# Two conditioned layers, fp32, on one core: another order of work where level 0 gives way to level 1, plain fp32 edge layers, and VectorE's fold step ahead of layer 1's in level 1

## The chip, the cores and the metric

One core of a Trainium2 chip. The metric is the device time of one launch in microseconds. The time before is a median of 933.09 us over 3 runs (the lowest 931.63, the highest 933.41).

## The reference, cut to what matters

```python
def _layer(x, style, w, b, mw, mb, typ):
    s = style @ mw.T + mb
    weight = SCALE * w * s[:, None, :, None]
    demod = lax.rsqrt(jnp.sum(weight * weight, axis=(2, 3)) + EPS)
    weight = weight * demod[:, :, None, None]
    ...
x = x + _L0_ffn_ref(_L0_cond_ref(x, cond_512, ...), L0_ffn_A, L0_ffn_B, L0_ffn_Wr)
x = x + _L1_ffn_ref(_L1_cond_ref(x, cond_512, ...), qweight, scales, zeros, bias)
```

x is 32 samples of 64 channels by 1024 positions, in fp32. The four layers of a level are of the types same, upsample (and blur), same, (blur and) downsample. Each of the two levels runs four modulated convolutions of three taps along the positions (64 channels in and out) and then a product along the positions: level 0's is a gated low-rank adapter (the top 16 of 64 experts by score), level 1's a matrix of 4-bit weights, unpacked as scale times nibble minus zero.

## The kernel before, in words

**Pairs.** The 32 samples are worked on in 16 pairs; a pair fills 128 rows in the products along positions. Level 0 handles pairs 0 to 15 and level 1 the same samples again as 16 to 31. `c` in the code is the pair whose convolutions are computed, `i` or `f` the pair whose product is; in level 0 `c = i + 1`, in level 1 `c = i + 3` (AHEAD). Level 0 stores its result in `x_after_first`, from which level 1 loads it again.

**Two parts for one fp32.** Most products run in the faster fp32r form on operands that are cut in two, hi and lo, and three matmuls (hi by hi, hi by lo, lo by hi) make one product (`products`, L175). ScalarE makes the hi part, VectorE the lo part by a subtraction (`low`, L164), and TensorE waits for the lo part. So nearly every step of a pair is a relay: TensorE, ScalarE (`act_...`), VectorE (`dve_...`), TensorE (`pe_...`).

**Steps of one pair c.** `split`: x into `x_hi`, `x_lo`. `layer1`: the first convolution into `conv_ps`, then `h_hi`, `h_lo`. `fold_start`, `fold3`, `fold2`: the weights of layers 2 to 4 are multiplied into one stationary operand for each sample, `v` (ScalarE `v_hi`, VectorE `v_lo`) then `r` (out of `fold_ps`, `r_hi` L755, `r_lo` L760) then `e` (`e_hi` L788 to L791, `e_lo` and two copies). `cond`: the product of `h` and `e`, four taps of three matmuls for each of the two samples, then ScalarE writes it out (L860). `pe_fold2(c)` waits for VectorE's `r_lo` of c and for `e` of c-1; `pe_cond(c, a)` for `e` of c and `h_lo`; `pe_layer1(c, a)` for VectorE's `x_lo` of c and for ScalarE's write of `cond(c-1, a)`.

**The edges.** The folded operand is wrong at the first and the last position of a sample. Those are computed apart, for all 32 samples together and one time in a level, by four small layers in a row: `edge_tensor` layer 0 to 3 on TensorE (widths 192, 128, 192 and 32 columns), and `edge_vector` step 0 to 4 on VectorE around them. Level 0 does that at the start of the program with raw fp32 operands (`head_edge_tensor`, `head_edge_vector`: one matmul for each product). Level 1 does it in the change of level with three fp32r matmuls for each product; its turn, w2 and down weights are cut in hi and lo by ScalarE (`edge_tiles`), GpSimd (`blurred_lo`) and VectorE (`raw_lo`), and each of its steps 0 to 3 ends with two VectorE instructions for the hi and lo part (`parts`). Step 0 needs the few end positions of all samples in `x_edge`: 30 samples come by DMA, the last two, which exist last, by eight small VectorE copies (`edge_copies`, L279 to L288), which raise `edges_copied`.

**Who waits for `edges_copied`.** SyncE, before it issues the three loads of scales, zeros and bias (L1228, 512 KB each), behind which the loads of `x_in` for pair 19 and all later ones stand in its queue (L1166, L1167); GpSimd's queue, before the loads of the first three residuals (L1280, 512 KB each); ScalarE, before nibbles 6 and 7.

**Order.** The order of all engines is written out by hand. The change of level is the stretch between level 0's loop and level 1's: pairs c = 17, 18 and 19 get their convolutions, level 0's last product runs in two halves (`pe_adapter_out`), and the 4-bit matrix is unpacked by VectorE and ScalarE in eight parts (`dve_nibbles`, `act_nibbles`). After it, `second_step(i)` runs for i = 17 to 28: on TensorE layer 1 of sample 0, transposes, layer 1 of sample 1, fold 3, a third of the quantized product, fold 2, two thirds of the product, `cond`. On VectorE it is:

```python
dve_turn(v, i, bufs)
dve_layer1(v, c, 0, bufs)
dve_fold3(v, c, bufs)
dve_layer1(v, c, 1, bufs)
dve_fold2(v, c, bufs)
```

Of the kernel before, what the change touches and what calls it, by code (L numbers as in the profile page):

```python
# [8 lines left out]
F32R = mybir.dt.float32r  # L9
# [11 lines left out]
P = 128  # L21
# [14 lines left out]
AHEAD = 3  # L36
# [4 lines left out]
def program(nc, t):  # L41
    with ExitStack() as outer:
# [52 lines left out]
        S.tiles_cleared = sem("tiles_cleared")  # L95
        S.sides_cleared = sem("sides_cleared")
# [138 lines left out]
        def setup_edges(stack, L, s):  # L235

            T = lambda n, s, d=F32: tensor(stack, f"L{L}_{n}", s, d)
            s.w2_raw, s.turn = T("w2_raw", [P, 2 * P]), T("turn", [P, 8, C])
            s.x_edge = T("x_edge", [P, 2, B, 4])
            if not L:  # L240
                s.edge = [T("side0", [P, 2, 4, B]), T("side1", [P, 2, 3, B]), T("side2", [P, 2, 4, B])]
                s.scaled, s.turned = T("side_scaled", [P, 2, 3, B]), T("side_turned", [P, 2, 2, 2, B])
                return
            s.w2_hi, s.w2_lo = T("w2_hi", [P, 2, P], F32R), T("w2_lo", [P, 2, P], F32R)
            s.turn_hi, s.turn_lo = T("turn_hi", [P, 4, P], F32R), T("turn_lo", [P, 4, P], F32R)
            s.down_hi, s.down_lo = T("down_hi", [P, 5 * C], F32R), T("down_lo", [P, 5 * C], F32R)
            s.edge, s.edge_hi, s.edge_lo = [None] * 4, [None] * 4, [None] * 4
            for i in range(2):
                n = 4 - i
                s.edge[i], s.edge_hi[i], s.edge_lo[i] = T(f"side{i}", [P, 2, n, B]), T(f"side_hi{i}", [P, 2, n, B], F32R), T(f"side_lo{i}", [P, 2, n, B], F32R)  # L250
                s.edge[i + 2], s.edge_hi[i + 2], s.edge_lo[i + 2] = s.edge[i], s.edge_hi[i], s.edge_lo[i]
            s.scaled = T("side_scaled", [P, 2, 3, B])
# [148 lines left out]
        def head_edge_tensor(pe, s, layer):  # L401
# [10 lines left out]
            pe.wait_ge(S.edge_ready, layer + 1)  # L412
            if layer in (0, 2):
                if layer:
                    pe.wait_ge(S.w2_loaded, 16)
                raw = s.w2_raw if layer else s.w1_raw
                last = sums(sides(prod_ps[0], 3), [raw[:, i * P:(i + 1) * P] for i in range(2)], [part(layer, i, 3) for i in range(2)])
            elif layer == 1:
                pe.wait_ge(S.turn_blurred, 1)
# [11 lines left out]
        def head_edge_vector(v, s, step):  # L431
# [9 lines left out]
            if step == 0:  # L441
                v.wait_ge(S.edges_loaded, 16)
                for side in range(2):
                    last = V.tensor_tensor(s.edge[0][:, side, :, :], s.x_edge[:, side, :, :].rearrange("p b j -> p j b"),
                                           wide(style_tab[:, 0, :], 4), ALU.mult)
                last.then_inc(S.edge_ready, 1)
            if step == 1:
                v.wait_ge(S.edge_done, 1)
                v.wait_ge(S.tables_ready, 1)
                v.wait_ge(S.sides_cleared, 1)  # L450
                link(v, V.scalar_tensor_tensor(out=six(s.scaled), in0=blocks(prod_ps[0], 6), scalar=SCALE, in1=wide(scale1, 6), op0=ALU.mult, op1=ALU.mult))
# [4 lines left out]
            if step == 2:  # L456
                v.wait_ge(S.edge_done, 2)
# [1443 lines left out]
```

## Time and profile before

| | us |
|---|---|
| median of 3 runs (931.63 to 933.41) | 933.09 |
| the profiled execution's own time | 933.7 |
| its span | 932.0 |
| TensorE busy in it | 918.5 |
| weight loads (PEld) busy | 826.8 |
| VectorE, ScalarE, GpSimd busy | 494.2, 410.0, 92.1 |

The 1.7 us between the profiled execution's time and its span lie before and after the first and the last instruction. In a timeline the ends of matmuls are modelled and overlap the next start, so the time that a group of matmuls takes is read from its first start to the start of what follows. "L" in front of a number is a line of the kernel before; in a tile name of the profile, "L_" stands for a buffer of either level.

### The profile page before, as it was taken

How to read it: one execution, taken by the hardware profiler on the slowest of the kernel's cores; microseconds unless marked ns; L12 is line 12 of the kernel's file. 1: busy time of each engine (PE TensorE's matmuls, PEld its weight loads, DVE VectorE, ACT ScalarE, POOL GpSimd, SP SyncE). 2: the span in 40 equal slices, each digit the busy share in tenths (PEclk: the TensorE clock that was granted, in tenths of full speed). 3: DMA queues.
4: the chain of work that ended last, by engine and by line, in shares of the span. 5: the costliest groups of instructions: out<-in, count | busy, mean ns of one | idle time of the engine just before them, and what ended most of it. 6: DMA issues, size and time to landing. Idle time of an engine off the chain costs nothing.

```text
span 932.0 us, 14652 instructions
## 1 busy us (share of the span) xinstructions
PE 918.5 (99%) x5032; PEld 826.8 (89%) x5032; DVE 494.2 (53%) x1071; ACT 410.0 (44%) x764; POOL 92.1 (10%) x115
## 2 busy tenths in 40 slices
PE   7899999999999999999999999999999999999998
PEld 6789899899899898898898898988998899998998
DVE  6795345245245244254344365587566556666555
ACT  4863333343244144233234234486555565555540
POOL 0000000000000000000000020321211121111121
PEclk9999999999999999999999999999999999999999
DMA  8802101101101011011012011334222221122111
GB/s 288 268 1 69 46 23 68 45 23 68 30 37 68 23 45 68 23 45 68 23 45 68 23 57 46 63 96 131 69 68 91 90 90 68 68 73 86 68 68 69
DMA packets 33004, 64.29 MB, mean 69 GB/s; under 512 B 11728, under 2 KB 13776, under 8 KB 32976
## 3 DMA queue, kind: packets, MB, share of 16 engines
q1 hardware_dynamic: 23904, 30.90, 11.1%
q0 software_dynamic: 9072, 33.03, 9.5%
q8 instruction: 16, 0.26, 0.1%
q14 instruction: 12, 0.10, 0.0%
HBM read 47.14 MB, written 16.78 MB: 69 GB/s over the span
## 4 chain that ended last, share of the span: by engine, by line
PE 92%; DVE 4%; ACT 2%; issue 1%; DMA 0%; DVEq 0%; ACTq 0%
PE conv_ps L180 9%; PE conv_ps L182 9%; PE conv_ps L181 9%; PE fold_ps L776 6%; PE prod_ps L966 5%; PE prod_ps L967 5%; PE prod_ps L968 5%; PE prod_ps L933 5%; PE prod_ps L935 5%; PE prod_ps L934 5%; PE prod_ps L1042 4%; PE prod_ps L1041 4%; PE fold_ps L741 3%; PE turn_ps L887 3%; PE turn_ps L935 2%; PE turn_ps L933 2%
## 5 line engine op out<-in xcount | busy, mean ns | idle before, releaser
L166 DVE TENSOR_TENSOR h_lo<-conv_ps,h_hi 64x512 fp32r<-64x512 f32 x128 | 88.3, 689 | 47.2 <-ACT h_hi L840 46.1
L180 PE MATMUL conv_ps<-h_hi,e_hi 128*128 128x512 f32 x256 | 104.1, 407 | 3.0 <-ACT e_hi L791 2.5
L181 PE MATMUL conv_ps<-h_lo,e_hi 128*128 128x512 f32 x256 | 102.6, 401 | 0.0
L182 PE MATMUL conv_ps<-h_hi,e_lo 128*128 128x512 f32 x256 | 102.4, 400 | 0.0
L860 ACT ACTIVATE cond<-conv_ps,bias,demod_tab 128x510 f32<-128x510 f32 x64 | 49.8, 778 | 105.7 <-PE conv_ps L182 103.1
L966 PE MATMUL prod_ps<-b_hi,xt 128*128 128x512 f32 x240 | 93.5, 390 | 0.0
L967 PE MATMUL prod_ps<-b_lo,xt 128*128 128x512 f32 x240 | 93.4, 389 | 0.0
L968 PE MATMUL prod_ps<-b_hi,xt 128*128 128x512 f32 x240 | 93.4, 389 | 0.0
L933 PE MATMUL prod_ps<-a_hi,xt 128*128 128x384 f32 x240 | 81.1, 338 | 0.0
L935 PE MATMUL prod_ps<-a_hi,xt 128*128 128x384 f32 x240 | 81.1, 338 | 0.0
L934 PE MATMUL prod_ps<-a_lo,xt 128*128 128x384 f32 x240 | 81.0, 338 | 0.0
L1041 PE MATMUL prod_ps<-quant,xt_hi 128*128 128x342 f32 x256 | 80.6, 319 | 0.0
L1042 PE MATMUL prod_ps<-quant,xt_lo 128*128 128x342 f32 x256 | 80.4, 320 | 0.0
L893 ACT ACTIVATE xt<-turn_ps 128x512 fp32r<-128x512 f32 x32 | 17.4, 595 | 143.1 <-PE turn_ps L887 143.0
L978 ACT ACTIVATE xt<-turn_ps 128x512 fp32r<-128x512 f32 x32 | 17.4, 595 | 135.4 <-PE turn_ps L942 135.4
L166 DVE TENSOR_TENSOR xt<-turn_ps,xt 128x512 fp32r<-128x512 f32 x64 | 41.2, 686 | 65.8 <-ACT xt L978 48.9
L820 DVE SCALAR_TENSOR_TENSOR x_lo<-x_in,style_tab,x_hi 128x513 fp32r<-128x513 f32 x64 | 45.8, 757 | 55.1 <-ACT x_hi L811 55.1
L1026 DVE SCALAR_TENSOR_TENSOR res<-prod_ps,norm,res 128x512 f32<-128x512 f32 x32 | 23.9, 751 | 95.0 <-PE prod_ps L968 92.9
L180 PEld LDWEIGHTS conv_ps<-h_hi,e_hi 128*128 128x128 f32 x256 | 48.9, 191 | 13.3 <-ACT e_hi L791 2.6
L182 PEld LDWEIGHTS conv_ps<-h_hi,e_lo 128*128 128x128 f32 x256 | 49.1, 192 | 11.4
L181 PEld LDWEIGHTS conv_ps<-h_lo,e_hi 128*128 128x128 f32 x256 | 49.0, 191 | 9.4
L166 DVE TENSOR_TENSOR xt_lo<-turn_ps,xt_hi 128x512 fp32r<-128x512 f32 x32 | 20.6, 686 | 63.4 <-ACT xt_hi L893 63.4
(299 smaller groups left out, 2162.8 us busy)
## 6 DMA issues: line engine op xcount, KB each, us to landing
x_in<-in_x SPq DMA_DIRECT2D x64, 128.0 KB, 2.7
res<-in_x POOLq DMA_DIRECT2D x16, 512.0 KB, 3.5
x_after_first<-res POOLq DMA_DIRECT2D x16, 512.0 KB, 2.9
x_in<-x_after_first SPq DMA_DIRECT2D x64, 128.0 KB, 2.7
res<-x_after_first POOLq DMA_DIRECT2D x16, 512.0 KB, 3.6
out_x<-res POOLq DMA_DIRECT2D x15, 512.0 KB, 3.0
a_raw<-in_adapter_in SPq DMA_DIRECT2D x8, 544.0 KB, 8.4
b_raw<-in_adapter_out SPq DMA_DIRECT2D x8, 512.0 KB, 8.2
```

What stands on the lines that cost most here:

```text
L166: return nc.vector.tensor_tensor(out, whole, hi.bitcast(F32), ALU.subtract)
L180: nc.tensor.matmul(out, hi(w), moving_hi(i), start=(i == 0), stop=False)
L181: nc.tensor.matmul(out, hi(w), moving_lo(i), start=False, stop=False)
L182: last = nc.tensor.matmul(out, lo(w), moving_hi(i), start=False, stop=(i == n - 1))
L933: nc.tensor.matmul(out, bufs.xt_hi[:, k, :], bufs.a_hi[:, k, cols], start=(k == 0), stop=False)
L934: nc.tensor.matmul(out, bufs.xt_hi[:, k, :], bufs.a_lo[:, k, cols], start=False, stop=False)
L935: last = nc.tensor.matmul(out, bufs.xt_lo[:, k, :], bufs.a_hi[:, k, cols], start=False, stop=(k == KT - 1))
L966: nc.tensor.matmul(prod_ps[n][:, :], bufs.xt_hi[:, k, :], bufs.b_hi[:, k, cols], start=(k == 0), stop=False)
L967: nc.tensor.matmul(prod_ps[n][:, :], bufs.xt_hi[:, k, :], bufs.b_lo[:, k, cols], start=False, stop=False)
L968: last = nc.tensor.matmul(prod_ps[n][:, :], bufs.xt_lo[:, k, :], bufs.b_hi[:, k, cols], start=False, stop=(k == KT - 1))
L1041: nc.tensor.matmul(out, bufs.xt_hi[:, k, :], bufs.quant[:, k, cols], start=(k == 0), stop=False)
L1042: last = nc.tensor.matmul(out, bufs.xt_lo[:, k, :], bufs.quant[:, k, cols], start=False, stop=(k == KT - 1))
```

## The change

It has four parts.

1. **Edge layers 1 to 3 of level 1 use raw fp32 operands.** `edge_tensor`, `edge_vector` and `edge_tiles` are gone; level 0's functions, renamed `plain_edge_tensor` and `plain_edge_vector`, serve both levels. Layer 0 stays in three fp32r matmuls for each product. Gone with it: ScalarE's three activations for hi parts, GpSimd's two subtractions, VectorE's subtraction for w2, and the hi and lo pairs behind steps 1 to 3. New: one ScalarE activation that lays `down` out flat (`down_flat`), and three memsets on VectorE.
2. **In the change of level** layer 1 of a pair goes in front of its fold 2 (TensorE, ScalarE, VectorE) for c = 18 and 19; edge layer 0 goes behind layer 1 of pair 18, edge layer 1 between the two halves of `cond(18)`, edge layer 2 in front of layer 1 of sample 1 of pair 19.
3. **VectorE's edge copies** go from the place right behind the last residual of level 0 to one behind the splits and fold 3 of pair 18; nibbles 6 and 7 go behind the splits of pair 19 on VectorE, and behind `cond(18, 0)` on ScalarE.
4. **In level 1's steps** VectorE's fold 3 goes ahead of layer 1 of sample 0.

The core of the diff:

```diff
@@ pe, change of level
             pe_cond(pe, c, 0, slot(c))
             pe_cond(pe, c, 1, slot(c))
+            c = NPAIR + 2
+            pe_layer1(pe, c, 0, slot(c))
+            pe_fold2(pe, c, slot(c))
+            pe_layer1(pe, c, 1, slot(c))
             pe.wait_ge(S.x1_ready, 2 * NPAIR + 1)
-            edge_tensor(pe, 1, set1, 0)
-            c = NPAIR + 2
+            plain_edge_tensor(pe, 1, set1, 0)
+            pe_fold3(pe, c + 1, slot(c + 1))
+            pe_cond(pe, c, 0, slot(c))
+            plain_edge_tensor(pe, 1, set1, 1)
+            pe_cond(pe, c, 1, slot(c))
+            i, c = NPAIR, NPAIR + AHEAD
+            pe_layer1(pe, c, 0, slot(c))
             pe_fold2(pe, c, slot(c))
-            pe_layer1(pe, c, 0, slot(c))
-            edge_tensor(pe, 1, set1, 1)
+            plain_edge_tensor(pe, 1, set1, 2)
             pe_layer1(pe, c, 1, slot(c))
-            pe_fold3(pe, c + 1, slot(c + 1))
-            for a in range(2):
-                pe_cond(pe, c, a, slot(c))
-            i, c = NPAIR, NPAIR + AHEAD
-            pe_fold2(pe, c, slot(c))
-            pe_layer1(pe, c, 0, slot(c))
-            edge_tensor(pe, 1, set1, 2)
-            pe_layer1(pe, c, 1, slot(c))
-            edge_tensor(pe, 1, set1, 3)
+            plain_edge_tensor(pe, 1, set1, 3)
@@ act, change of level
             act_cond(act, c, 0, slot(c))
+            act_cond(act, c, 1, slot(c))
+            c = NPAIR + 2
+            act_fold_start(act, c + 1, slot(c + 1))
+            act_layer1(act, c, 0, slot(c))
+            act_fold2(act, c, slot(c))
+            act_layer1(act, c, 1, slot(c))
+            act_fold3(act, c + 1, slot(c + 1))
+            split(c + 1, slot(c + 1))
+            act_cond(act, c, 0, slot(c))
             act.wait_ge(S.edges_copied, 1)
             act_nibbles(act, 6, KT)
             act_cond(act, c, 1, slot(c))
...
@@ v, change of level
             dve_first_residual(v, f, buf0)
+            dve_layer1(v, c, 1, slot(c))
+            c = NPAIR + 2
+            split(c, slot(c))
+            dve_fold3(v, c, slot(c))
             edge_copies(v, set1, buf0)
+            plain_edge_vector(v, 1, set1, 0)
+            dve_fold_start(v, c + 1, slot(c + 1))
+            dve_layer1(v, c, 0, slot(c))
+            dve_fold2(v, c, slot(c))
             dve_layer1(v, c, 1, slot(c))
-            edge_vector(v, 1, set1, 0)
+            dve_fold3(v, c + 1, slot(c + 1))
+            plain_edge_vector(v, 1, set1, 1)
+            c = NPAIR + AHEAD
+            split(c, slot(c))
             dve_nibbles(v, 6, KT)
...
+            plain_edge_vector(v, 1, set1, 2)
+            dve_layer1(v, c, 0, slot(c))
             dve_fold2(v, c, slot(c))
-            edge_vector(v, 1, set1, 3)
-            dve_layer1(v, c, 0, slot(c))
-            edge_vector(v, 1, set1, 4)
+            plain_edge_vector(v, 1, set1, 3)
+            plain_edge_vector(v, 1, set1, 4)
             dve_layer1(v, c, 1, slot(c))
@@ v, second_step
                 dve_turn(v, i, bufs)
+                dve_fold3(v, c, bufs)
                 dve_layer1(v, c, 0, bufs)
-                dve_fold3(v, c, bufs)
                 dve_layer1(v, c, 1, bufs)
```

How instructions stand now, at three places (the changed kernel has its own line numbers). First TensorE in the change of level, only the first matmul of each group; x_in's tiles are layer 1, r_hi fold 2, v_hi fold 3, h_hi cond, L_side the edges. Before, behind `cond(17, 1)`:

```order
L180 MATMUL prod_ps<-L_side_hi,w_hi 128x192 [waits lo_w1,edge_ready,x1_ready]
...
L776 MATMUL fold_ps<-r_hi,fold_hi 128x256 [waits fold2_ready,fold2_hi,fold3_ready]
...
L180 MATMUL conv_ps<-x_hi,w_hi 128x512 [waits cond_out,xin_split]
...
L180 MATMUL prod_ps<-L_side_hi,L_turn_hi 128x128 [waits lo_turn,edge_ready]
...
L741 MATMUL fold_ps<-v_hi,fold_hi 128x384 [waits fold3_ready,fold_in_ready]
```

And now, from the same place:

```order
L181 MATMUL conv_ps<-x_hi,w_hi 128x512 [waits cond_out,xin_split]
...
L691 MATMUL fold_ps<-r_hi,fold_hi 128x256 [waits fold2_ready,fold2_hi,fold3_ready]
...
L181 MATMUL prod_ps<-L_side_hi,w_hi 128x192 [waits edge_ready,x1_ready]
...
L656 MATMUL fold_ps<-v_hi,fold_hi 128x384 [waits fold3_ready,fold_in_ready]
...
L402 MATMUL prod_ps<-L_side,L_turn 128x128 [waits turn_blurred,edge_ready]
```

Pair 18's layer 1 and fold 2 stand ahead of edge layer 0 now, and edge layer 1 stands behind fold 3 and `cond(18, 0)`.

Second, VectorE around the edge copies. Before:

```order
L287 COPY L_x_edge<-res 64x4
L166 TENSOR_TENSOR h_lo<-conv_ps,h_hi 64x512 [waits layer1_hi]
...
L640 TENSOR_TENSOR L_side<-L_x_edge,style_tab 128x128 [waits edges_copied,edges_loaded]
...
L760 SCALAR_TENSOR_TENSOR r_lo<-fold_ps,scale,r_hi 128x4x64 [waits fold3_hi]
...
L820 SCALAR_TENSOR_TENSOR x_lo<-x_in,style_tab,x_hi 128x513 [waits xin_hi,layer1_done,xin_loaded0]
```

Now:

```order
L167 TENSOR_TENSOR h_lo<-conv_ps,h_hi 64x512 [waits layer1_hi]
...
L735 SCALAR_TENSOR_TENSOR x_lo<-x_in,style_tab,x_hi 128x513 [waits xin_hi,layer1_done,xin_loaded0]
...
L675 SCALAR_TENSOR_TENSOR r_lo<-fold_ps,scale,r_hi 128x4x64 [waits fold3_hi]
...
L277 COPY L_x_edge<-res 64x4 [waits edges_clear,x1_ready]
...
L442 TENSOR_TENSOR L_side<-L_x_edge,style_tab 128x128 [waits edges_copied,edges_loaded]
```

The copies moved behind `h_lo` of (17, 1), both splits and the fold step of pair 18.

Third, VectorE in level 1's step. Before, and then now:

```order
L166 TENSOR_TENSOR h_lo<-conv_ps,h_hi 64x512 [waits layer1_hi]
L166 TENSOR_TENSOR h_lo<-conv_ps,h_hi 64x512
L758 REGISTER_ALU
L760 ISA [waits fold3_hi]
L760 SCALAR_TENSOR_TENSOR r_lo<-fold_ps,scale,r_hi 128x4x64
```

```order
L675 ISA [waits fold3_hi]
L675 SCALAR_TENSOR_TENSOR r_lo<-fold_ps,scale,r_hi 128x4x64
L675 ISA
L675 SCALAR_TENSOR_TENSOR r_lo<-fold_ps,scale,r_hi 128x4x64
L758 REGISTER_ALU
L167 TENSOR_TENSOR h_lo<-conv_ps,h_hi 64x512 [waits layer1_hi]
```

The two `r_lo` stand ahead of both `h_lo` of sample 0.

## Rows read from the trace of the kernel before

**Rows 1.** The page, busy time of each engine (us, share of the span, instructions).
```profile
PE 918.5 (99%) x5032; PEld 826.8 (89%) x5032; DVE 494.2 (53%) x1071; ACT 410.0 (44%) x764; POOL 92.1 (10%) x115
```

**Rows 2.** Waits in 656 to 905 us: engine, tile, line, releaser, us, times, longest.
```profile
PEld fold_ps L776 <- DVE r_lo L760: 2.6, 12, 0.2
```

**Rows 3.** Timeline, ScalarE and VectorE in one level-1 step (start us, length us, engine, line).
```profile
669.39 0.84 ACT L755 ACTIVATE r_hi<-fold_ps,scale 128x256 fp32r<-128x256 f32 x2
...
669.29 1.39 DVE L166 TENSOR_TENSOR h_lo<-conv_ps,h_hi 64x512 fp32r<-64x512 f32 x2 [1.07 <-ACT h_hi L840]
...
670.71 0.88 DVE L760 SCALAR_TENSOR_TENSOR r_lo<-fold_ps,scale,r_hi 128x256 fp32r<-128x256 f32 x2
```

**Rows 4.** Timeline, TensorE in the change of level.
```profile
623.28 0.39 PE L182 MATMUL conv_ps<-h_hi,e_lo 128*128 128x512 f32 x1
...
624.18 0.50 PE L180 MATMUL conv_ps<-h_hi,e_hi 128*128 128x512 f32 x1 [0.51 <-DVE h_lo L166]
...
627.07 0.26 PE L180 MATMUL prod_ps<-L_side_hi,w_hi 128*128 128x192 f32 x1
...
627.95 0.38 PE L776 MATMUL fold_ps<-r_hi,fold_hi 128*128 128x256 f32 x1
...
631.25 0.33 PE L180 MATMUL prod_ps<-L_side_hi,L_turn_hi 128*128 128x128 f32 x1
...
632.64 0.45 PE L180 MATMUL conv_ps<-x_hi,w_hi 128*128 128x512 f32 x1
...
645.82 0.40 PE L182 MATMUL conv_ps<-x_hi,w_lo 128*128 128x512 f32 x1
...
646.49 0.28 PE L180 MATMUL prod_ps<-L_side_hi,L_down_hi 128*128 128x32 f32 x1 [0.28 <-DVE L_side_lo L166]
...
648.52 0.48 PE L180 MATMUL conv_ps<-h_hi,e_hi 128*128 128x512 f32 x1
...
656.70 0.31 PE L1041 MATMUL prod_ps<-quant,xt_hi 128*128 128x342 f32 x1
```

**Rows 5.** Windows: length, busy of five engines, PEclk, DMA share, GB/s.
```profile
28.20:31.60 3.40, 3.40 (x9) 2.29 (x7) 2.37 (x8) 1.88 (x3) 0.00 (x0) 0.50 1.03 411
...
628.00:636.00 8.00, 8.00 (x49) 6.89 (x50) 6.80 (x17) 7.00 (x13) 0.00 (x0) 1.00 1.03 359
...
649.30:653.00 3.70, 3.70 (x11) 2.84 (x10) 1.21 (x2) 0.64 (x6) 3.63 (x2) 0.54 0.00 0
```

**Rows 6.** Waits in 24 to 32 us, same columns as rows 2.
```profile
PE conv_ps L180 <- ACT e_hi L791: 2.5, 1, 2.5
```

**Rows 7.** Timeline, TensorE at the program's start, level 0's edge layers 1 and 3.
```profile
21.52 1.05 PE L409 MATMUL prod_ps<-L_side,L_turn 128*128 128x128 f32 x8
...
22.33 0.37 PE L776 MATMUL fold_ps<-r_hi,fold_hi 128*128 128x256 f32 x1
...
35.56 1.42 PE L409 MATMUL prod_ps<-L_side,L_down 128*128 128x32 f32 x12
...
36.81 0.48 PE L180 MATMUL conv_ps<-x_hi,w_hi 128*128 128x512 f32 x1
```

**Rows 8.** Timeline, ScalarE in the change of level.
```profile
629.05 0.79 ACT L722 ACTIVATE v_hi<-down_T,scale 128x192 fp32r<-128x192 f32 x2
...
629.97 0.60 ACT L788 ACTIVATE e_hi<-fold_ps 128x512 fp32r<-128x512 f32 x1
...
634.36 0.75 ACT L837 ACTIVATE conv_ps<-conv_ps,bias,scale 128x512 f32<-128x512 f32 x1 [0.73 <-PE conv_ps L182]
...
637.16 1.39 ACT L811 ACTIVATE x_hi<-x_in,style_tab 128x513 fp32r<-128x513 f32 x2
```

**Rows 9.** Timeline, VectorE, last of the edge copies.
```profile
622.46 0.17 DVE L287 COPY L_x_edge<-res 64x4 f32<-64x4 f32 x1
```

**Rows 10.** Timeline, SyncE's DMA issues in the change of level.
```profile
624.32 0.33 SPq L1228 DMA_DIRECT2D scales<-in_L_ffn_scales  x1
...
629.41 0.50 SPq L1166 DMA_DIRECT2D x_in<-x_after_first  x1
```

More of the change, by code:

```diff
@@ L239, in setup_edges @@
             s.x_edge = T("x_edge", [P, 2, B, 4])
[L240 to L252, printed above, removed]
+            if L:
+                s.edge_hi, s.edge_lo = T("side_hi0", [P, 2, 4, B], F32R), T("side_lo0", [P, 2, 4, B], F32R)
+                s.down_flat = T("down_flat", [P, 5 * C])
+            s.edge = [T("side0", [P, 2, 4, B]), T("side1", [P, 2, 3, B]), T("side2", [P, 2, 4, B])]
+            s.scaled, s.turned = T("side_scaled", [P, 2, 3, B]), T("side_turned", [P, 2, 2, 2, B])
         mod_b = lambda s, l: s.cols[:, l:l + 1]
@@ L410, in sums @@
                 return last
-            pe.wait_ge(S.edge_ready, layer + 1)
-            if layer in (0, 2):
+            pe.wait_ge(S.edge_ready, 4 * L + layer + 1)
+            if L and layer == 0:
+                rounded = lambda w: (lambda i: w[:, :, i:i + 3, :].rearrange("p s j b -> p s (j b)"))
+                last = products(sides(prod_ps[0], 3), (0, 1), tiles(w1_hi), tiles(w1_lo), rounded(s.edge_hi), rounded(s.edge_lo))
+            elif layer in (0, 2):
                 if layer:
-                    pe.wait_ge(S.w2_loaded, 16)
+                    pe.wait_ge(S.w2_loaded, 16 * (L + 1))
                 raw = s.w2_raw if layer else s.w1_raw
@@ L445, in head_edge_vector @@
                                            wide(style_tab[:, 0, :], 4), ALU.mult)
+                if L:
+                    flat = lambda w: w[:, :, :, :].rearrange("p s j b -> p (s j b)")
+                    link(v, last)
+                    link(v, V.tensor_copy(flat(s.edge_hi), flat(s.edge[0])))
+                    last = low(flat(s.edge_lo), flat(s.edge[0]), flat(s.edge_hi))
                 last.then_inc(S.edge_ready, 1)
             if step == 1:
[L448 to L451, printed above, removed]
+                v.wait_ge(S.edge_done, 4 * L + 1)
+                v.wait_ge(S.tables_ready, L + 1)
+                link(v, V.scalar_tensor_tensor(out=six(s.scaled), in0=blocks(prod_ps[0], 6), scalar=1.0 if L else SCALE, in1=wide(scale1, 6), op0=ALU.mult, op1=ALU.mult))
                 for side, rows, src, dst in ((0, lo_half, slice(0, 3), slice(0, 3)), (0, hi_half, slice(0, 2), slice(1, 3)),
@@ L1271, in _ @@
             blur_turn(pool, 1, set1)
-            for group in ("turn", "down"):
-                blurred_lo(pool, 1, set1, group)
             pool.wait_ge(S.x1_ready, 2 * NPAIR + 1)
```

151 lines of the change are left out of this document (28 added, 123 removed).

## The prediction, blind

> **What bounds the kernel now.** The page's busy times come first [rows 1]: TensorE is busy for 918.5 us, 99% of the span, the others for 53% at most. So a change can only win by a wait of TensorE, by its own work, or by its clock; work of the other engines counts where TensorE waits for its result. I read next the waits of TensorE in level 1's loop [rows 2]: one kind stands there 12 times, fold 2 waiting for VectorE's `r_lo`, 2.6 us together. The timeline of the two feeding engines [rows 3] shows why. ScalarE's `r_hi` of both samples ends at 670.23, but VectorE is in `h_lo` until 670.68 and `r_lo` ends at 671.59. Last I read TensorE's timeline in the change of level [rows 4], measuring each group from its first start to the next group's, and the granted clock there [rows 5].
>
> **Part 4, the loop.** With fold 3 in front, `r_lo` starts when `r_hi` is there, about 670.24, and ends at 671.12, 0.47 earlier [rows 3]. The wait is 2.6 / 12 = 0.2 a step [rows 2], so all of it goes. `h_lo` of sample 0 ends 0.88 - 0.4 = about 0.5 later. It is read by `cond`, which stands behind two thirds of the quantized product and is not waited for in the rows of waits; that cover holds. Price: -2.4 us, a little under 2.6, as the record of the weight loader counts some time that the matmuls hide.
>
> **Part 1, plain fp32.** Edge layer 1 takes 632.64 - 631.25 = 1.39 now and layer 3 takes 648.52 - 646.49 = 2.03 [rows 4]. The same layers with raw operands took 22.33 - 21.52 = 0.81 and 36.81 - 35.56 = 1.25 at the start of the program [rows 7]: -0.58 and -0.78; layer 2 is even to 0.05. With restarts in the old ones I take **-1.4 us** of TensorE work. The page "FP8 and Floating Point Precision" of the Trainium skill (TensorE Precision Notes) says the opposite of such an edit: true fp32 takes four passes of the array where the cut operands take three products. By it the four and six products would be 16 and 24 passes of 0.11 us, 1.8 and 2.6 instead of 0.8 and 1.25, and the edit would cost 1.0 instead of bringing 1.4. The trace does not agree: each plain product has two records there, and the time of the group is under that of the cut one. On ScalarE and GpSimd the work that goes is off the path; it makes ScalarE's chain in front of `h_hi` of pair 17 some 0.2 earlier at most.
>
> **Part 3, the copies.** Before, the last ended at 622.63 [rows 9], ahead of the landing of the last stored sample, so SyncE issued the constants at 624.32 [rows 10] and lost nothing by the copies. Now the copies stand behind `h_lo` of (17, 1) (about 623.6), two splits of 0.72, `r_lo` of 0.88 and 1.6 of their own: they end at about 627.7. The three constants and three residuals, 512 KB each, start 3.4 us later. The loads of `x_in` for pair 19 stand behind the constants in the same queue, and they need the split of pair 18, which is earlier, so they are issued no later than 629.41 [rows 10]. But the DMA engines are full in 628 to 636 [rows 5], with those six transfers before anything of `x_in`; ScalarE's `x_hi` of pair 19 began at 637.16 [rows 8], 7.8 after the issue. With the same 3 MB started 3.4 later I expect it at **about 640.5**. Before, ScalarE had other work until then; now it has its `cond(17)`, fold steps and layer 1 of pair 18 done by about 634.8, and behind the blocked `x_hi` stand the write of `cond(18, 0)`, nibbles 6 and 7, `cond(18, 1)` and the hi parts of pair 19.
>
> **Part 2, the order in the change of level.** I wrote out all three engines' new order with lengths from the rows (cond 2.80, layer 1 half of it, fold 2 1.72, fold 3 1.06 on TensorE; h_lo 1.39, r_lo 0.88 on VectorE; `v_hi` 0.79, `e_hi` three of 0.60, two-part layer 1 2.0 on ScalarE [rows 3, 4, 8]), started from the times of before at 604 us, and carried each wait forward. The same working with the old order gives back the trace's times within 0.3 us. TensorE's waits in the new one:
> - `cond(17, 1)` for `h_lo`: 0.15 (0.67 before: 624.18 - 623.28 less a matmul of 0.23).
> - `cond(18, 0)` for VectorE's `e_lo`: 0.4.
> - Edge layer 1 for VectorE's step 1: **1.7**. From the end of `cond(17, 1)` the relay is 0.2 + cond out 0.7, `v_hi` 0.7, layer 1 2.0, `e_hi` 1.8 and layer 1 2.0 on ScalarE, then `h_lo` 1.4, `r_lo` 0.9, step 1 1.4 on VectorE: 11.1. TensorE has 1.4 + 1.7 + 1.4 + 0.65 + 1.06 + 2.8 = 9.0 and the 0.4 of the wait above.
> - Layer 1 of (19, 0) for the write of `cond(18, 0)`, behind the late load: 1.2.
> - Edge layer 2: 0.45.
> - Edge layer 3 for VectorE's step 3: **3.5**. Behind it stand ScalarE 2.0, `h_lo` 1.4, `e_lo` copies 1.5 and step 3 0.8 after layer 1 of (19, 0), against 1.7 + 0.6 + 1.4 on TensorE; that alone is 2.3, and the rest comes from nibbles and `cond` that ScalarE does late.
>
> Sum of the new waits 7.4, and 0.1 at each of six restarts (a first matmul's record is 0.50 long instead of 0.39 [rows 4]): +8.0. The old waits that go: 0.67, 0.44 in front of edge layer 3 (646.49 - 645.82 less 0.23), 0.23 in front of fold 2 (627.95 - 627.07 less six matmuls of 0.11), restarts 0.3 [rows 4]: -1.6. With the edge work -1.4 the change of level is **+5.0** at full clock. Nearest rows as bounds: no new wait at all would make it -3.0; late load twice as bad, +7.
>
> **The clock.** It falls to 0.54 in 649.3 to 653.0 [rows 5], the lower level of 1.2 GHz, and costs 1.6 us: TensorE had just done edge layer 3 of 32-column matmuls after a short wait. At the start of the program it fell to 0.50 [rows 5] behind a wait of 2.5 us [rows 6]. The new order has a wait of 3.5 in front of a shorter edge layer 3, so I expect it to fall once again, for about 3 us: +1.4 new, -1.6 old.
>
> Sum: +5.0 - 0.2 - 2.4 = +2.4. The last `cond` of the change of level ends 4.5 later by the time stamps of my working than in the old order without the clock's fall, which makes it +1.9 (short waits overlap with what the rows count into groups); I take **+2.1**. The profiled execution goes from 933.7 (span 932.0 and 1.7 around it) to 935.8. That execution was 0.6 over the median of 933.09, so the median goes to **935.2**.
>
> **Rivals.**
> 1. **The load is not late in effect.** The x_in loads share the engines with the residuals, and the constants may be through sooner. Then edge layer 3 waits 2.3, and layer 1 of pair 19 and edge layer 2 not at all: 2.9 less of waits, some 1.4 by time stamps instead of 4.5, and 1.4 - 0.2 - 2.4 = -1.2: **931.9**. For it: the amount is the same, and the last of it decides. Against: 359 GB/s in a window already full. It decides if `x_hi` starts before 638.
> 2. **Faster: the clock stays up.** As 1, and the waits, split in several short ones, don't bring the fall; the old fall goes, -1.6 with no +1.4, so -1.2 - 1.4 = -2.6: **930.5**. For it: the plain layer has fewer and longer matmuls than the 18 short ones after which it fell. Against: the wait of 2.5 behind which it fell at the start [rows 6]. It decides if every wait stays under some 2 us.
> 3. **The loop gains nothing.** Fold 2 is released by `r_lo`, but `h_lo` 0.5 later makes `cond` or the split wait, 12 times 0.2, so 2.1 + 2.4: **937.6**. Against: two thirds of the quantized product between them.
> That the change moves something else than it says is excluded by the order of the instructions.
>
> **Chances.** Forecast 0.60, own range 933.6 to 936.6 (load 1 us earlier or later, the clock's 1.4 once or not); rival 1 0.18, rival 2 0.12, rival 3 0.10. Range 931.2 to 937.2, leaving out most of rival 2 and half of rival 3. About 0.2%, 1.9 us, can be told from no change: 931.2 to 935.0 is "same". Same holds rival 1 and 0.25 of the forecast, slower its other 0.35 and rival 3, faster rival 2 and a little of 1: 0.13, 0.42, 0.45.
>
> **What the profile of the changed kernel would show.** Loop: no wait of fold 2 for `r_lo` (part 4 right). SyncE's constants issued at 627 to 628 and `x_hi` of pair 19 starting at 640 to 641 (part 3 right; before 638, rival 1). TensorE's waits: about 1.7 in front of edge layer 1 and 3 to 4 in front of edge layer 3, then a clock near 0.5 for some 3 us. Plain edge layers of 0.8 and 1.25. First third of the quantized product of pair 16 at about 661, 4 to 5 later than 656.70 [rows 4]. I am wrong if that start is before 658.5, or if the loop from there on is not 2 to 2.6 shorter.

## The result, and the profile after

| | us |
|---|---|
| median before, 5 runs (931.32 to 933.41) | 931.77 |
| median of the change, 5 runs (936.39 to 937.54) | 936.52 |
| ratio, with its 95% interval | 1.0047 (1.0034 to 1.0060) |
| profiled execution of the change, and its span | 937.54, 935.7 |

The change makes the kernel slower by 4 to 5 us. The forecast was 935.2, with the sign right; against the profiled execution of before it forecast 2.1 more, and 3.8 more was measured (937.5 against 933.7), so the size of the loss was forecast at about half. The page of the change: TensorE has less to do than in [rows 1], and the span is longer.

```profile
PE 916.8 (98%) x5020; PEld 827.3 (88%) x5020; DVE 489.5 (52%) x1062; ACT 408.8 (44%) x762; POOL 89.2 (10%) x113
```

To see where the time went I cut both traces at the same three places in TensorE's work: the first matmul of fold 2 of pair 17, the first matmul of the quantized product of pair 16, and the first one of pair 31. Timeline of TensorE, before (the middle cut is 656.70 in [rows 4]):

```profile
609.66 0.28 PE L776 MATMUL fold_ps<-r_hi,fold_hi 128*128 128x256 f32 x1
...
920.69 0.32 PE L1041 MATMUL prod_ps<-quant,xt_hi 128*128 128x342 f32 x1
```

And of the change, with the waits between the first two cuts:

```profile
609.23 0.28 PE L691 MATMUL fold_ps<-r_hi,fold_hi 128*128 128x256 f32 x1
...
622.85 0.39 PE L183 MATMUL conv_ps<-h_hi,e_lo 128*128 128x512 f32 x1
623.22 0.50 PE L181 MATMUL conv_ps<-h_hi,e_hi 128*128 128x512 f32 x1
...
632.15 0.34 PE L656 MATMUL fold_ps<-v_hi,fold_lo 128*128 128x384 f32 x1
632.82 0.47 PE L181 MATMUL conv_ps<-h_hi,e_hi 128*128 128x512 f32 x1 [0.33 <-issue]
...
635.46 0.39 PE L183 MATMUL conv_ps<-h_hi,e_lo 128*128 128x512 f32 x1
637.10 1.16 PE L402 MATMUL prod_ps<-L_side,L_turn 128*128 128x128 f32 x8 [1.25 <-DVE L_side L456]
...
640.66 0.39 PE L183 MATMUL conv_ps<-h_hi,e_lo 128*128 128x512 f32 x1
642.26 0.47 PE L181 MATMUL conv_ps<-x_hi,w_hi 128*128 128x512 f32 x1 [1.21 <-ACT cond L775]
...
647.60 0.40 PE L183 MATMUL conv_ps<-x_hi,w_lo 128*128 128x512 f32 x1
651.38 2.77 PE L402 MATMUL prod_ps<-L_side,L_down_flat 128*128 128x32 f32 x12 [3.39 <-DVE L_side L473]
653.96 0.77 PE L181 MATMUL conv_ps<-h_hi,e_hi 128*128 128x512 f32 x1
...
658.76 1.11 PE L802 MATMUL turn_ps<-ident,cond 128*128 128x128 f32 x8
...
662.50 0.31 PE L956 MATMUL prod_ps<-quant,xt_hi 128*128 128x342 f32 x1
...
924.51 0.32 PE L956 MATMUL prod_ps<-quant,xt_hi 128*128 128x342 f32 x1
```

| stretch | before | change | difference |
|---|---|---|---|
| to fold 2 of pair 17 | 609.66 | 609.23 | -0.43 |
| change of level, to the first quantized product | 47.04 | 53.27 | +6.23 |
| loop, to the last one | 263.99 | 262.01 | -1.98 |
| after it, to the end of the span | 11.31 | 11.19 | -0.12 |

The 0.43 at the head does not come of the change: in two profiles of one kernel, both without a fall of the clock, this cut lies at 609.17 and 608.74 (the variant with step 3 ahead, below). The loop gained nearly what was forecast, and the change of level lost more. A start in these rows less the start above it, less the 0.23 of a 512-column matmul or the 0.17 of a 384-column one, is the wait: 0.50 in front of `cond(18, 0)`, 1.41 in front of edge layer 1, 1.37 in front of layer 1 of (19, 0), 3.55 in front of edge layer 3. With 0.14 for `cond(17, 1)` and 0.21 for edge layer 2 (its lines are not shown) the waits come to 7.2. The rows also show edge layer 3 taking 653.96 - 651.38 = 2.58 instead of 1.25 [rows 7], and `cond(19, 0)` 658.76 - 653.96 = 4.80 for twelve matmuls instead of 2.80. The windows say why (length, busy of five engines, PEclk, DMA share, GB/s):

```profile
651.90:653.60 1.70, 1.70 (x10) 1.70 (x9) 0.00 (x0) 0.00 (x0) 0.00 (x0) 0.50 0.00 0
653.60:658.30 4.70, 4.70 (x13) 3.80 (x13) 1.77 (x4) 0.68 (x6) 3.46 (x2) 0.51 0.00 2
```

The clock is at its lower level, 1.2 GHz, from the start of edge layer 3 on, for about 6.8 us (a window from 651.38 to 658.20 has 0.50 too). In [rows 5] a mean of 0.54 over 3.7 us makes that 3.4 us.

The load was late, as forecast in kind. SyncE's and ScalarE's timeline:

```profile
627.07 0.33 SPq L1143 DMA_DIRECT2D scales<-in_L_ffn_scales  x1
...
628.72 0.51 SPq L1081 DMA_DIRECT2D x_in<-x_after_first  x1
...
638.59 0.73 ACT L726 ACTIVATE x_hi<-x_in,style_tab 128x513 fp32r<-128x513 f32 x1 [4.29 <-DMA x_in<-x_after_first]
640.73 0.72 ACT L726 ACTIVATE x_hi<-x_in,style_tab 128x513 fp32r<-128x513 f32 x1 [1.41 <-DMA x_in<-x_after_first]
```

The constants leave 2.75 later than in [rows 10], and ScalarE stands for 4.29 and 1.41 us waiting for `x_in` of pair 19. And VectorE's relay in front of edge layer 3:

```profile
647.61 1.39 DVE L167 TENSOR_TENSOR h_lo<-conv_ps,h_hi 64x512 fp32r<-64x512 f32 x2 [1.99 <-ACT h_hi L755]
649.03 0.69 DVE L167 TENSOR_TENSOR e_lo<-fold_ps,e_hi 128x512 fp32r<-128x512 f32 x1
...
650.97 0.36 DVE L473 TENSOR_TENSOR L_side<-L_side_scaled,L_bias 128x192 f32<-128x192 f32 x1
```

Step 3 (ended 651.33) stands behind `h_lo` and the whole `e_lo`.

### The profile page after: what moved, and what is told of

Read it like the earlier page. It is cut to its first block, busy times and chain, and to the rows that moved or that the text cites. A ratio compares the mean times of both kernels' runs of the same rounds, so it can differ in the third digit from the quotient of the medians.

```text
span 935.7 us, 14616 instructions
## 1 busy us (share of the span) xinstructions
PE 916.8 (98%) x5020; PEld 827.3 (88%) x5020; DVE 489.5 (52%) x1062; ACT 408.8 (44%) x762; POOL 89.2 (10%) x113
## 4 chain that ended last, share of the span: by engine, by line
PE 91%; DVE 3%; ACT 3%; DMA 1%; issue 1%; SPq 0%; DVEq 0%; ACTq 0%
PE conv_ps L181 9%; PE conv_ps L183 9%; PE conv_ps L182 9%; PE prod_ps L881 5%; PE prod_ps L882 5%; PE prod_ps L883 5%; PE fold_ps L691 5%; PE prod_ps L848 5%; PE prod_ps L850 5%; PE prod_ps L849 5%; PE prod_ps L957 4%; PE prod_ps L956 4%; PE fold_ps L656 3%; PE turn_ps L802 3%; PE turn_ps L850 2%; PE turn_ps L848 2%
## 5 line engine op out<-in xcount | busy, mean ns | idle before, releaser
L181 PE MATMUL conv_ps<-x_hi,w_hi 128*128 128x512 f32 x128 | 53.3, 417 | 1.2 <-ACT cond L775 1.2
```

The source lines that it names most:

```text
L181: nc.tensor.matmul(out, hi(w), moving_hi(i), start=(i == 0), stop=False)
```

## The experiments

Each variant was timed beside the kernel before, in three sessions with one baseline each; the third has one execution of each kernel and is not in the table. "Stretch" is the change of level as cut above, in the profiled execution. The mean granted clock of an execution turned out to be needed to read the times. Where there is a profile, 1.000 goes with no fall of the clock, 0.998 with one of about 3.4 us, 0.996 with two of 3.4 or one of 6.8, and 0.994 with one of each. Executions of one kernel fall into groups by it. Where an execution has no profile, its falls are read from this value alone.

| kernel | median | before beside it | ratio (95%) | stretch | executions by mean clock: mean us |
|---|---|---|---|---|---|
| before | 933.45 | | | 47.04 | 10 at 1.000: 931.65; 2 at 0.998: 933.01; 23 at 0.996: 933.73 |
| change again | 937.79 | 933.63 | 1.0039 (1.0026 to 1.0052) | 53.51 | 2 at 0.996: 936.91; 3 at 0.994: 938.04 |
| loop only | 931.50 | 933.45 | 0.9982 (0.9974 to 0.9991) | 47.10 | 11 at 0.995 to 0.997, 9 of them at 0.996: 931.72 |
| plain only | 931.58 | 933.45 | 0.9982 (0.9974 to 0.9991) | 44.39 | 10 at 0.998: 931.54; 1 at 0.999 |
| load first | 932.90 | 933.45 | 0.9998 (0.9985 to 1.0012) | 47.11 | 6 at 1.000: 931.21; 6 at 0.994: 934.96 |
| fill | 934.82 | 933.45 | 1.0018 (1.0009 to 1.0027) | 50.27 | 11 at 0.997 to 0.999 |
| copies back | 934.55 | 933.63 | 1.0007 (0.9995 to 1.0018) | 48.63 | 3 at 0.999 to 1.000: 931.48; 1 at 0.996; 8 at 0.994: 934.83 |
| step 3 ahead | 932.37 | 933.63 | 0.9981 (0.9972 to 0.9990) | 46.01 | 4 at 1.000: 930.25; 7 at 0.996: 932.58 |
| old order, plain, loop | 928.68 | 933.63 | 0.9949 (0.9937 to 0.9962) | 44.46 | 2 at 1.000: 928.59; 3 at 0.997 to 0.998: 929.17 |

**The change once more.** No edit.

> The changed kernel itself, unaltered, on the chip and in the session of the variants. Theory A: 4.0 to 4.8 us over the kernel before's median, and every execution has a fall of the clock in the change of level (mean granted clock 0.996, as the five executions shown have), since the wait of 3.5 us is there in each. Rival (the fall is a matter of chance in each execution, as it looks to be after the 2.3 us wait): some executions at a mean clock of 0.998 to 1.000, about 3.4 us faster than the others.

All five executions have a fall; none is near 933.4. By their mean clocks (0.996 twice, 0.994 three times) three have a further one, which the expectation did not have; the profile, at 0.994, shows it at the program's start. The stretch repeats within 0.24 us, the wait of 3.55 to the hundredth. The rival is out for this kernel.

**Part 4 alone, on the kernel before.**

```diff
@@ v, second_step
                 dve_turn(v, i, bufs)
+                dve_fold3(v, c, bufs)
                 dve_layer1(v, c, 0, bufs)
-                dve_fold3(v, c, bufs)
                 dve_layer1(v, c, 1, bufs)
```

> The kernel before with part 4 alone (VectorE's fold step ahead of layer 1's in level 1's steps). Theory A (the four parts add up: loop about -2.0 us, change of level +6.2, as the two profiles show from the first quantized product to the last): this kernel is 1.8 to 2.2 us under the kernel before, and the wait of fold 2 for r_lo is gone, 12 steps of about 0.16 each. Rival (the loop's 2.0 us in the profile of the change belong to how it enters the loop later and with other loads under way, not to the new order): within 0.5 us of the kernel before.

Its stretch is the old one, and its loop is 262.02 us long instead of 263.99:

```profile
656.43 0.31 PE L1041 MATMUL prod_ps<-quant,xt_hi 128*128 128x342 f32 x1
...
918.45 0.32 PE L1041 MATMUL prod_ps<-quant,xt_hi 128*128 128x342 f32 x1
```

At the same mean clock of 0.996 the executions are 933.73 - 931.72 = 2.0 apart. Twelve steps, 0.16 each. The wait named in [rows 2] is gone from the answer on waits; what stands there for `r_lo` is VectorE waiting for ScalarE:

```profile
DVE r_lo L760 <- ACT r_hi L755: 25.3, 12, 2.2
```

**Part 1 alone.** The changed kernel's edge functions, with the order of before everywhere (TensorE, ScalarE, VectorE and the copies as in the lines with a minus in the diff of the change).

> The kernel before with part 1 alone (plain fp32 edge layers 1 to 3, old order everywhere). Theory A: TensorE's edge layers 1 and 3 take 0.81 and 1.25 instead of 1.39 and 2.03, and the waits stay: -1.4 us, and the clock falls behind edge layer 3 as before. Rival (the fall of the clock hangs on the 18 short matmuls of the old edge layer 3): the clock stays up, -3.0 us. Second rival (plain fp32 takes four passes of the array against three products): +1.0 us.

Its stretch is 2.65 shorter than before. 1.6 of that is the fall of the clock behind edge layer 3, which is absent in this profile. It is absent in the other ten executions too, as far as the mean clock tells: none has the 0.996 that two falls give. So about 1.0 is the edge layers, less than the 1.4 of TensorE's work in them: `cond(18, 0)` and `cond(19, 0)` now wait about 0.7 each for their `h_lo`, more than what the shorter waits elsewhere give back. One of these is the wait of `cond(17, 1)`: it is 0.15 here (623.26 - 622.88 less 0.23) instead of 0.67, so its loss belongs to part 1 and not to the new order. The fall went away as the rival had it; whether for the fewer matmuls or for the shorter wait in front of them (0.44 before, none now) this run does not tell. The four-pass rival is out: edge layer 1 takes 0.81 here, as expected, and the stretch is shorter and not longer.

**The load ahead of the constants.**

```diff
@@ sp
+            sp.wait_ge(S.xin_split, 2 * (NPAIR + 2) + 2)
+            sp_load(sp, NPAIR + 3, False)
             sp.wait_ge(S.x1_stored, 16 * NPAIR)
             sp.wait_ge(S.edges_copied, 1)
@@
-            with sp.Fori(NPAIR + 2, END - 1) as i:
+            with sp.Fori(NPAIR + 3, END - 1) as i:
```

> The changed kernel, with SyncE's four loads of x_in for pair 19 issued ahead of the three constants. Theory A (late load costs the wait of layer 1 of pair 19 and about 1.2 of the 3.55 in front of edge layer 3; the rest of that wait is the relay itself): x_hi of pair 19 starts with no wait for its load, no wait of layer 1 (19, 0), 2.3 us in front of edge layer 3; 2.6 to 3.1 us under the changed kernel, so about 1.7 to 2.2 over the kernel before; the clock still falls. Rival B (the load is late but the relay would have been too): under 0.8 us gained. Rival C (the clock falls for as long as it does because of the 3.5 us of waiting; a wait of 2.3 doesn't bring it down): another 3.4 gained, so about 1.4 under the kernel before.

The waits came to the hundredth: none in front of layer 1 of (19, 0), and 648.31 - 645.78 - 0.23 = 2.30 in front of edge layer 3. TensorE's timeline of this execution, which had no fall:

```profile
645.78 0.40 PE L183 MATMUL conv_ps<-x_hi,w_lo 128*128 128x512 f32 x1
648.31 1.53 PE L402 MATMUL prod_ps<-L_side,L_down_flat 128*128 128x32 f32 x12 [2.13 <-DVE L_side L473]
649.67 0.48 PE L181 MATMUL conv_ps<-h_hi,e_hi 128*128 128x512 f32 x1
...
656.31 0.31 PE L956 MATMUL prod_ps<-quant,xt_hi 128*128 128x342 f32 x1
```

So rival B falls, and of theory A and rival C each holds in half of the executions: the times stand in two groups 3.75 us apart, six at a clock of 1.000 and six at 0.994. A second profile of the same kernel was to show the other group.

**The same kernel, a second profile.** No edit.

> The variant with the load ahead of the constants once more, for a profile of an execution in which the clock falls (6 of 12 had 0.994 and 935.0 us, 6 had 1.000 and 931.2). Theory A: same waits (1.4 and 2.3 us) as in the execution at full clock, and a fall behind the one of 2.3 that costs 3.0 to 3.5 us of TensorE's time in edge layer 3 and cond(19, 0). Rival: the waits themselves are longer in such an execution (a later load).

It took 934.78 us at 0.994. TensorE's timeline:

```profile
645.91 0.40 PE L183 MATMUL conv_ps<-x_hi,w_lo 128*128 128x512 f32 x1
648.44 2.77 PE L402 MATMUL prod_ps<-L_side,L_down_flat 128*128 128x32 f32 x12 [2.13 <-DVE L_side L473]
651.02 0.77 PE L181 MATMUL conv_ps<-h_hi,e_hi 128*128 128x512 f32 x1
...
655.84 1.11 PE L802 MATMUL turn_ps<-ident,cond 128*128 128x128 f32 x8
...
659.57 0.31 PE L956 MATMUL prod_ps<-quant,xt_hi 128*128 128x342 f32 x1
```

Its windows at the program's start and behind the wait, and the first profile's behind the wait:

```profile
20.00:35.00 15.00, 12.50 (x61) 10.28 (x60) 11.19 (x34) 11.66 (x18) 0.74 (x1) 0.89 1.01 363
...
648.60:650.00 1.40, 1.40 (x8) 1.40 (x8) 0.00 (x0) 0.00 (x0) 0.00 (x0) 0.50 0.00 0
650.00:655.00 5.00, 5.00 (x15) 4.14 (x16) 1.76 (x4) 0.68 (x6) 3.10 (x2) 0.50 0.00 2
```

```profile
649.60:652.60 3.00, 3.00 (x16) 2.48 (x16) 1.76 (x4) 0.68 (x6) 2.07 (x1) 1.00 0.01 3
```

The wait is the same 2.13 in both. Edge layer 3 takes 2.58 here and 1.36 there, and the stretch from fold 2 of pair 17 is 50.29 against 47.11: **3.2 us is the price of this fall by itself**, with nothing else changed. It is the cleanest number for what the clock cost the change, whose own rows give the same: 2.58 - 1.36 and 4.80 - 2.80, 3.2 together. The two profiled executions are 934.78 - 931.59 = 3.2 apart too, so nothing else differs between them, though this one also has a fall at the program's start (0.89 in 20 to 35 us): fold 2 of pair 17 starts at 609.28 here and at 609.20 there. What makes the other 0.6 between the two groups' means is not shown.

The groups show one thing more. Six executions have both falls and six have none, and not one has a single fall. So the falls of an execution are not independent of each other; the cause is open.

**Filling the wait.** The 18 matmuls are extra work whose result is overwritten.

```diff
@@ pe, change of level
             pe_layer1(pe, c, 1, slot(c))
+            for n in range(18):
+                nc.tensor.matmul(prod_ps[1][:, 0:6 * C], w1_hi[:, n % 2, :], fold2_hi[:, :], start=True, stop=True)
             plain_edge_tensor(pe, 1, set1, 3)
```

> The changed kernel with 18 matmuls of 384 columns on constant tiles, result unused, put in the wait ahead of edge layer 3 (about 3.1 of the 3.55 us; they are extra work and give nothing to the output). Theory A and C alike (the clock fell to half because TensorE waited; edge layer 3 took 2.58 instead of 1.25 and cond(19, 0) 4.8 instead of 2.9): the clock stays at full and the time is 3.2 to 3.4 us under the changed kernel, about 1.4 over the kernel before. Rival D (the fall comes of the short 32-column matmuls of edge layer 3 or of where it lies in time, not of the wait): no gain, the clock falls around edge layer 3 all the same.

TensorE's timeline (L1336 are the extra matmuls):

```profile
648.78 3.31 PE L1336 MATMUL prod_ps<-fold_hi,w_hi 128*128 128x384 f32 x18
652.34 1.52 PE L402 MATMUL prod_ps<-L_side,L_down_flat 128*128 128x32 f32 x12 [0.25 <-DVE L_side L473]
653.70 0.48 PE L181 MATMUL conv_ps<-h_hi,e_hi 128*128 128x512 f32 x1
```

And the window behind the wait, in the columns of [rows 5]:

```profile
652.00:656.00 4.00, 3.75 (x23) 3.24 (x23) 2.05 (x5) 0.89 (x7) 1.44 (x1) 1.00 0.01 2
```

Edge layer 3 starts no earlier than it would (it hangs on VectorE), but it and `cond` run at full clock, the stretch is 3.0 shorter than in the change, and no execution is under 0.997. By the medians against the baselines, useless work in the wait gains 2 to 3 us (ratios of 1.0039 and 1.0047 without it, 1.0018 with it): the fall came of the wait. Rival D is out. The gain is under the 3.2 to 3.4 expected; the two kernels were timed in different sessions.

**The copies put back.**

```diff
@@ v, change of level
             dve_first_residual(v, f, buf0)
+            edge_copies(v, set1, buf0)
             dve_layer1(v, c, 1, slot(c))
@@
             dve_fold3(v, c, slot(c))
-            edge_copies(v, set1, buf0)
             plain_edge_vector(v, 1, set1, 0)
```

> The changed kernel with VectorE's edge copies put back to where they were (right behind the last residual). Theory A (the copies hold the constants and the residuals, and so x_in of pair 19): constants issued near 624.3 again, x_hi of pair 19 starts at 637 to 637.7, no wait of layer 1 (19, 0), 2.3 in front of edge layer 3; cond(17, 1) waits about 0.5 more for h_lo. In all 2.4 to 2.9 us under the changed kernel where the clock falls alike. Rival B (order in SyncE's queue alone decides, so the start of the constants does not matter): load as late as in the changed kernel, no gain, 0.5 lost.

SyncE's and ScalarE's timeline. The constants left early again, and `x_hi` of pair 19 came even earlier than expected:

```profile
624.04 0.33 SPq L1143 DMA_DIRECT2D scales<-in_L_ffn_scales  x1
...
625.69 0.50 SPq L1081 DMA_DIRECT2D x_in<-x_after_first  x1
...
635.93 0.73 ACT L726 ACTIVATE x_hi<-x_in,style_tab 128x513 fp32r<-128x513 f32 x1 [0.95 <-DMA x_in<-x_after_first]
```

ScalarE waits 0.95 and 0.77 for the two samples, and the write of `cond(18, 0)` behind them is in time: no wait of layer 1 (19, 0), 2.30 in front of edge layer 3: with the constants still first in the queue the load is in time if they start early. That the new place of the copies is what made the load late is shown from both sides. What of it is the later issue and what the full DMA queues is not: the loads of `x_in` are issued at 625.69 here and at 628.72 in the change, behind the constants both times, and landed 8.7 to 9.6 us later here and 8.5 to 9.8 in the change. The median is 3.2 us under that of the change in the same session; where the clock falls, at 0.994, it is 938.04 - 934.83 = 3.2 too, a little over the 2.4 to 2.9 expected. The wait of `cond(17, 1)` did not grow by 0.5, as was expected; it is 0.11.

The profile, at a mean clock of 0.996, also bears on the clock. Behind edge layer 3's wait:

```profile
650.00:655.00 5.00, 5.00 (x19) 4.15 (x19) 1.76 (x4) 0.68 (x6) 3.43 (x2) 0.66 0.01 2
```

A mean of 0.66 over 5 us is 3.4 us at the lower level, and the stretch is 48.63 - 47.11 = 1.5 longer than in the load-first profile without a fall. So behind one and the same wait of 2.30 there was no fall, one of 3.4 us that cost 1.5, and one of 6.8 us that cost 3.2.

**Step 3 ahead.** On top of the load ahead of the constants:

```diff
@@ v, change of level
             plain_edge_vector(v, 1, set1, 2)
+            plain_edge_vector(v, 1, set1, 3)
             dve_layer1(v, c, 0, slot(c))
             dve_fold2(v, c, slot(c))
-            plain_edge_vector(v, 1, set1, 3)
```

> The changed kernel with the loads of pair 19 ahead of the constants (as in the earlier variant) and VectorE's edge step 3 put ahead of h_lo and the e_lo copies of pair 19. Theory A (the 2.3 us in front of edge layer 3 are VectorE's h_lo 1.4 and e_lo 1.5 that stand ahead of step 3): edge layer 3 waits about 0.2, cond(19, 0) about 1.2 for e_lo instead, 0.9 to 1.1 us less than that variant at the same clock; and with no wait over 1.4 us in the change of level its clock stays up in every execution. Rival C (the fall comes by the sum of the waits, not by one long one): some executions still at 0.994.

TensorE's timeline at edge layer 3 and the `cond` behind it:

```profile
646.05 1.42 PE L402 MATMUL prod_ps<-L_side,L_down_flat 128*128 128x32 f32 x12
...
648.57 0.47 PE L181 MATMUL conv_ps<-h_hi,e_hi 128*128 128x512 f32 x1 [1.09 <-issue]
```

Edge layer 3 does not wait, `cond(19, 0)` waits 1.3, and at a clock of 1.000 the kernel is 931.21 - 930.25 = 0.96 faster than with step 3 behind. But the clock did not stay up in every execution: seven of eleven have 0.996 and lie 2.3 us higher. Rival C's mark was 0.994, so it is not met in its words, but the expectation that with no wait over 1.4 us the clock stays up fell. A second profile was to show where the fall lies:

> The variant with step 3 ahead once more, for a profile of an execution in which the clock falls (7 of its 11 executions had a mean granted clock of 0.996 and took 932.6 us on average, 4 had 1.000 and 930.3; the profile taken was one of the latter). Theory A: the fall lies behind edge layer 3 and cond(19, 0) in the change of level, where TensorE has waited 1.2 twice within few us, and costs 1.6 to 2.3 us; the time from fold 2 of pair 17 to the first quantized product is then 47.6 to 48.3 instead of 46.0. Rival: the fall lies at the program's start only, and the stretch takes 46.0 again.

That execution had no fall either (929.75 us at 1.000), so the place of it stays open.

**The old order with plain edges and the new loop.** The part 1 kernel plus part 4: the change without parts 2 and 3.

> Parts 1 and 4 with the old order of the change of level and the copies in their old place: the changed kernel without parts 2 and 3. Theory A (gains of the two parts add: loop -2.0, plain edges -1.4 and, as they did alone, no fall of the clock at edge layer 3): no wait of edge layer 3 in the trace, 3.7 to 4.2 us under the kernel before's median, best of all so far. Rival (the two share the same slack): no better than either alone, -2.0.

TensorE's timeline, edge layers 2 and 3 and the first quantized product:

```profile
642.81 0.81 PE L402 MATMUL prod_ps<-L_side,L_w_raw 128*128 128x192 f32 x4
...
644.85 1.42 PE L402 MATMUL prod_ps<-L_side,L_down_flat 128*128 128x32 f32 x12
...
646.83 0.47 PE L181 MATMUL conv_ps<-h_hi,e_hi 128*128 128x512 f32 x1 [0.55 <-DVE h_lo L167]
...
653.43 0.31 PE L956 MATMUL prod_ps<-quant,xt_hi 128*128 128x342 f32 x1
```

Edge layer 3 has no wait; `cond(19, 0)` behind it has one of 0.6. This is the fastest version, 0.9949 of before and 4.95 us less at the median, more than the 3.7 to 4.2 expected. At a clock of 1.000 on both sides it is 931.47 - 928.59 = 2.9 less (1.0 from the edges, 2.0 from the loop); the rest are falls, which 20 of the 23 executions of before beside it have, most of them two. Three of its own five have one, a short one by their mean clocks of 0.997 and 0.998. The change as made is 9.1 us slower than the same change without parts 2 and 3. Its stretch of 44.46 is the reference for the sum: 53.27 - 44.46 = 8.8. Of this 3.2 are the clock's, and 2.96 the late load's (the difference of the change and the load-first variant, 53.27 - 47.11 = 6.2, less those 3.2). The last 2.65 are what the load-first variant still has over this one (47.11 - 44.46): the order, and the place of the copies apart from the load.

## Why the prediction was right or wrong, point by point

**Right: what bounds, and where the loss comes from.** The waits were forecast at 0.15, 0.4, 1.7, 1.2, 0.45 and 3.5 and measured at 0.14, 0.50, 1.41, 1.37, 0.21 and 3.55; the sum at 7.4, and measured at 7.2. The relay in front of edge layer 1 was shorter than worked out by 0.3. The 2.3 that the relay alone would leave in front of edge layer 3 was measured at 2.30, in both load-first profiles and in the copies-back one. That match is partly luck: the terms that the forecast wrote down for it make 2.0 (5.7 less 3.7), and the hand-overs between the engines, which it left out, are the rest. The wait of `cond(17, 1)` came at 0.14 against 0.15, but for another reason than the order, since part 1 alone takes it away; the forecast gave part 1 some 0.2 at most there.

**Right: the late load.** Forecast for 640.5, from constants that start at 627.7. They started at 627.07, and the two samples' `x_hi` at 638.59 and 640.73, so the first was 1.9 earlier than forecast and outside the 640 to 641 named as the mark of part 3, and the second was inside. Both ways of taking the lateness away (the load first, the copies back) took the wait of layer 1 (19, 0) and 1.25 of that in front of edge layer 3. Rival 1, the load in time, is out: `x_hi` did not start before 638.

**Right in kind: plain fp32.** Layer 1 took 638.01 - 637.10 = 0.91 with a restart, forecast at 0.81; layer 3 took 1.36 at full clock with one, forecast at 1.25. Layer 2, called even to 0.05, took 0.51 in the part 1 kernel against 0.65. The Trainium skill ("FP8 and Floating Point Precision", TensorE Precision Notes) says that true fp32 takes four passes through the array; by the forecast's estimate from it layers 1 and 3 would have cost 1.0 more. The trace does not bear that out for layers of this size: 0.81 in the part 1 kernel against 1.39 before. Taken alone in the old order, the gain of part 1 at full clock is 1.0 and not 1.4, since new waits for `h_lo` appear there once the edges are quicker, and the old fall of the clock goes with it, 1.6 more. The forecast priced part 1 in the new order only.

**Slightly off: the loop.** -2.4 was taken from 2.6 in the row of waits. The measured gain is 2.0, in the change and alone (1.98 in the change, a hair outside the 2 to 2.6 that the forecast named as its mark). The start-to-start rows of the kernel before already held the answer: the excess in front of and behind fold 2's first matmul was 0.16 to 0.2 a step, and the row of waits, which is the weight loader's, counts a little that the matmuls before it cover. Rival 3 is out.

**Wrong in size: the clock.** The step "so I expect it to fall once again, for about 3 us: +1.4 new" failed. The fall was there, in all ten executions of the change, but in both profiles it lasted 6.8 us, over all of edge layer 3 and nearly all of `cond(19, 0)`, and cost 3.2. The term +1.4 was the mis-sized one. I had carried over the length of the old fall, which came behind a wait of 0.44, to one behind 3.55. Why it is twice as long is open: the wait alone does not set it, since behind 2.30 both lengths were seen. With 3.2 instead of 1.4 and 2.0 instead of 2.4, my sum of +2.4 becomes 2.4 + 1.8 + 0.4 = +4.6. The stretches show 6.23 - 1.98 = +4.25, and the medians +4.75 and +4.16 in the two sessions. The first quantized product started at 662.50 and not at about 661. That the forecast of 935.2 lies only 1.3 under 936.52 is luck: it was built on a median of 933.09, and the median of before in that comparison was 931.77.

**Wrong in kind: one execution for all.** The forecast set the fall of [rows 5] against every execution of before. Of 58 executions of before beside the variants, 13 have no fall at all and lie near 931.6, 41 have 0.996 and lie near 933.7, and 4 lie between. The change has a fall each time. So the difference of two medians hangs on how many of the quick ones a sample of before holds: 931.77 in the first comparison, which had three of five below 931.8, and 933.45 and 933.63 in the later ones. Rival 2 (the clock stays up) was in the end not about this kernel, but it is what half of the executions of the load-first variant do.

## What to carry to other kernels

When an order is rewritten so that a relay of three engines gets shorter for one step, write out all three engines' new order with times from the trace before believing it: all six waits were in that sheet to within 0.3 us, and it said that the new order loses. Take a change of several parts apart before judging it: two parts were worth 5 us here and the other two cost 9, most of it through one moved group of small copies that held a DMA queue, and through the clock. A wait of TensorE costs its own length, and it can cost a stretch at half clock on top, 1.5 to 3.2 us here; where the wait can't be removed, useless matmuls in it can pay, as they did here.

## What the runs showed of the hardware that I had not expected

- The same kernel with the same waits runs with and without a fall of TensorE's clock from one execution to the next. Behind 2.1 us of idle TensorE the clock fell in 6 of 12 executions of the load-first kernel and in 9 of 12 of the copies-back one, behind 3.4 us in 10 of 10, and with that wait filled in none of 11. All these counts go by the mean clock. No run here shows the cause. The Trainium skill ("TensorE: Matmul & The Clock Gate", Part 1: The HAM clock gate) says that what watches TensorE's activity runs freely and doesn't restart with a kernel. That would make it a matter of chance in each execution, which fits the groups but isn't shown by them.
- A fall has one of two lengths in these profiles: 3.4 us at half clock, which cost 1.5 or 1.6 in the change of level (the kernel before, copies back), or 6.8 us, which cost 3.2 (the change, load first). Behind the same wait of 2.30 us both were seen.
- Six transfers of 512 KB that started 3 us later made the small loads behind them land later, though those were issued at nearly the same time (628.72 instead of 629.41 [rows 10]): 8.5 to 9.8 us after their issue instead of 6.1 to 7.0, and 2.7 to 2.9 where they went ahead of the constants. The two samples landed at 638.5 and 640.6 instead of 637.1 and 637.7, which is 1.4 and 2.9 later.
